# Attention's squared scores as TensorE weights, with the norm as a 129th column, and outputs normed in rows before they are transposed and projected

## What is computed

```python
qk = jnp.einsum('bthd,bshd->bhts', q, k) * scale
a = qk ** DEG                                   # DEG = 2
gate = logG[:, :, :, None] - logG[:, :, None, :]
a = jnp.where(causal, a * jnp.exp(gate), 0.0)
norm = jnp.sum(a, axis=-1) + 1e-06
y = jnp.einsum('bhts,bshd->bthd', a, v)
y = y / jnp.transpose(norm, (0, 2, 1))[..., None]
return y.reshape(B, T, H * R * D) @ Wc + bc
```

## Time and profile before

| | |
|---|---|
| median of 3 runs | 2522.14 us (2518.66 to 2523.69) |
| the profiled execution, its time | 2519.12 us |
| its span, first to last instruction | 2517.2 us |
| TensorE matmul busy | 2289.9 us, 91% |
| GpSimd busy | 1535.7 us, 61% |
| VectorE busy | 1409.0 us, 56% |
| ScalarE busy | 1221.0 us, 49% |
| mean granted TensorE clock | 0.958 |
| attention's first and last L1162/L1159 | 58.5 us and 1765.2 us |

### The profile page before, as it was taken

The page is one execution under the profiler, slowest core; times in us unless marked ns, Lnnn a source line. Parts: engine busy times, 40 slices in busy tenths (PEclk is TensorE's granted clock), DMA queues, the critical chain, the costliest instruction groups (busy, mean ns, idle before and its releaser), DMA issues.

```text
span 2517.2 us, 34737 instructions
## 1 busy us (share of the span) xinstructions
PE 2289.9 (91%) x11880; PEld 1783.5 (71%) x11880; DVE 1409.0 (56%) x3036; ACT 1221.0 (49%) x2322; POOL 1535.7 (61%) x1422
## 2 busy tenths in 40 slices
PE   5999999999999899999989999998787999999980
PEld 3777776776767677676767767666576788888870
DVE  2444444445565444556544455654653878788863
ACT  3454444444434444443444444334333677777763
POOL 2666555544568754456875445687323688888885
PEclk8999999999999999999989999999788999999995
DMA  3766722122113212211321221121443988898956
GB/s 119 299 257 243 272 101 64 40 66 67 49 52 104 84 40 66 67 49 52 104 84 40 66 66 49 52 84 52 146 155 125 273 209 206 195 218 190 216 88 219
DMA packets 152695, 310.34 MB, mean 123 GB/s; under 512 B 26528, under 2 KB 88224, under 8 KB 152512
## 3 DMA queue, kind: packets, MB, share of 16 engines
q1 hardware_dynamic: 104176, 252.05, 29.8%
q0 software_dynamic: 48192, 55.68, 11.5%
q10 hardware_dynamic: 144, 0.33, 0.0%
HBM read 168.01 MB, written 149.34 MB: 126 GB/s over the span
## 4 chain that ended last, share of the span: by engine, by line
PE 71%; DVE 8%; POOL 8%; issue 7%; ACT 4%; DMA 2%; POOLq 0%; SPq 0%; ACTq 0%; DVEq 0%
PE bank L810 44%; PE bank L1162 13%; PE bank L820 6%; PE bank L1172 3%; POOL nacc L2038 3%; POOL slots L2077 2%; PE bank L1262 2%; POOL y_part L2087 2%; PE bank L1159 1%; DVE acc L1699 1%; DVE ub L1664 1%; ACT a L1415 1%; DVE yt_lo L1678 1%; ACT yt_hi L1426 1%; DMA y_part<-y_e,row_token 1%
## 5 line engine op out<-in xcount | busy, mean ns | idle before, releaser
L2038 POOL TENSOR_TENSOR nacc<-nacc,a 128x512 f32<-128x512 f32 (+1 forms) x384 | 448.0, 1167 | 292.1 <-ACT a L1419 139.8
L1162 PE MATMUL bank<-a,v 128*128 128x512 f32 x1024 | 529.0, 598 | 5.3 <-DVE nrm L1684 4.9
L2087 POOL DMA_INDIRECT y_part<-y_e,row_token x264 | 415.9, 1575 | 103.5 <-issue 82.5
L1415 ACT ACTIVATE a<-bank,c_s 128x512 f32<-128x512 f32 x384 | 263.4, 686 | 172.7 <-PE bank L810 148.5
L810 PE MATMUL bank<-q_hi,k_hi 128*128 128x512 f32 (+1 forms) x640 | 323.8, 506 | 12.5 <-ACT a L1415 6.2
L1419 ACT ACTIVATE a<-ub 128x512 f32<-128x512 f32 (+1 forms) x256 | 133.9, 523 | 392.2 <-DVE ub L1664 374.3
L2038 POOL TENSOR_TENSOR nacc<-a,a 128x512 f32<-128x512 f32 (+1 forms) x128 | 149.0, 1164 | 258.6 <-ACT a L1415 199.0
L1699 DVE SCALAR_TENSOR_TENSOR acc<-bank,rec,acc 128x256 f32<-128x256 f32 x512 | 223.5, 478 | 95.6 <-PE bank L810 89.6
L2077 POOL DMA_INDIRECT slots<-rows,slot_u x192 | 192.5, 1003 | 137.4 <-DVE slot_u L1826 86.1
L810 PE MATMUL bank<-q_lo,k_hi 128*128 128x512 f32 (+1 forms) x640 | 240.3, 375 | 0.0
L810 PE MATMUL bank<-q_hi,k_lo 128*128 128x512 f32 (+1 forms) x640 | 238.5, 373 | 0.0
(11 more groups left out here) (217 smaller groups left out, 5666.9 us busy)
## 6 DMA issues: line engine op xcount, KB each, us to landing
slots<-acc SPq DMA_DIRECT2D x65, 816.0 KB, 7.3
w_raw_f<-in_wffn SPq DMA_DIRECT2D x66, 624.0 KB
xr<-slots SPq DMA_DIRECT2D x64, 544.0 KB
decay_all<-decay_dram SPq DMA_DIRECT2D x128, 128.0 KB
w_hi<-w_dram SPq DMA_DIRECT2D x24, 384.0 KB
w_lo<-w_dram SPq DMA_DIRECT2D x24, 384.0 KB
sum<-y_part SPq DMA_DIRECT2D x16, 512.0 KB, 9.6
wc_hi<-wc_dram SPq DMA_DIRECT2D x24, 256.0 KB
```

Of the source, the lines that this page charges most:

```text
L1162: e.matmul(dst, v[n % 3][:, s, :], a32[u % NA][:, :, :], start=first, stop=False, skip_group_check=True).then_inc(s_av)
L1415: e.activation(squares, score_bank(u)[:, 0:R * w].rearrange("p (r t) -> p r t", r=R), ACT.Square, scale=c_s[b % 2][:, g * (g - 1) + s, h:h ...
L2038: e.tensor_tensor(out_, a, b, op).then_inc(s_nadd)
L2087: e.indirect_dma_start(out=y_part[part], out_offset=bass.IndirectOffsetOnAxis(ap=token, axis=0), in_=y_e[y][:, j, :], in_offset=None, boun ...
```

## The change

The sides of the second product are exchanged. The squares `a` are the weights, 128 query tokens at a time, and the moving side is `v` with a 129th column of ones (`DN = D + 1`). A full unit is now 4 products of 129 columns (two tiles of 128 tokens times R = 2), a half is 2. Outputs come in rows, tokens on the partitions, and the 129th column is the norm. A group takes two banks, so only two groups have a place at a time (`PLACE_OF`), and a group waits until the one before it in its place was read out by `normed`. The units' order is changed for that.

Gone are GpSimd's whole `av` (`nacc`), the norm's products on TensorE, ScalarE's `decay_f` and the copy `yt` from the outputs' bank. The decay is VectorE's product with one number a row, two instructions a group (`f_t`, made once a sequence). After a group's last unit VectorE adds the epsilon, takes the reciprocal and writes the normed rows `yn`; two units later TensorE transposes them (4 transposes into a spare bank), ScalarE and VectorE split them into `yt_hi` and `yt_lo`; and two units after that the 12 products of the projection run as one task, both query heads added up in one bank, which VectorE adds to `acc` in one instruction.

```diff
-UNITS = []
-for g_ in range(1, NG):
-    UNITS += [(g_, s_) for s_ in range(2 * g_)] + [(g_ - 1, 2 * g_ - 2), (g_ - 1, 2 * g_ - 1)]
-UNITS += [(NG - 1, 2 * NG - 2), (NG - 1, 2 * NG - 1)]
+
+UNITS = ([(0, 0), (0, 1)] + [(1, 0), (1, 1)] + [(2, 0), (2, 1)] + [(1, 2), (1, 3)] + [(2, 2), (2, 3)]
+         + [(3, s_) for s_ in range(6)] + [(2, 4), (2, 5)] + [(3, 6), (3, 7)])
...
+PLACE_OF, before_in = {}, {}
+free_ = [(0, None), (1, None)]
+for n_, g_, s_ in UNITS_ALL:
+    if (n_, g_) not in PLACE_OF:
+        PLACE_OF[n_, g_], before_in[n_, g_] = free_.pop(0)
+    if s_ == 2 * g_ + 1:
+        free_.append((PLACE_OF[n_, g_], (n_, g_)))
+
+DN = D + 1
...
-            do("yt", n_, g)
-            late += [(u + 2, "norm", n_, g, 0), (u + 2, "project", n_, g, 0), (u + 3, "project", n_, g, 1)]
+            do("normed", n_, g)
+            late += [(u + TURN_BEHIND, "turn", n_, g), (u + PROJECT_BEHIND, "project", n_, g)]
...
-        return GROUP_NTH[n - 1, g] + 1 if n else 0
+        return GROUP_NTH[before_in[n, g]] + 1 if before_in[n, g] else 0
...
-        def av_bank(g):
-            return bank[2 + g]
+        def outputs(n, g):
+
+            return banks[1 + PLACE_OF[n, g]][:, :, 0:R * DN].rearrange("p t (r d) -> p t r d", r=R)
...
             def av(u):
                 n, g, s = UNITS_ALL[u]
-                first = s == 0
-                dst = av_bank(g)[:, :].rearrange("p (r t) -> p r t", r=R)
+                dst = outputs(n, g)
                 once.wait_ge(s_sq, u + 1)
                 once.wait_ge(*out_of(("val", n // PAIR, s // 2)))
-                if first:
-
-                    once.wait_ge(s_nrm, place_free(n, g))
+                once.wait_ge(s_ones, 6)
+                if s == 0:
+
+                    once.wait_ge(s_yn, place_free(n, g))
                 if s == 2 * g and g:
-                    once.wait_ge(s_off, f_nth(n, g))
-                if s == 2 * g + 1:
-                    e.matmul(dst[:, :, P:GROUP], v[n % 3][:, s, :], a32[u % NA][:, :, 0:P], start=False, stop=True,
-                             skip_group_check=True).then_inc(s_av)
-                else:
-                    e.matmul(dst, v[n % 3][:, s, :], a32[u % NA][:, :, :], start=first, stop=False,
-                             skip_group_check=True).then_inc(s_av)
-
-            def norm(n, g):
+                    once.wait_ge(s_off, nth["decay", n, g])
+                for tt in range(s - 2 * g if s > 2 * g else 0, 2):
+                    t0 = tt * P if s <= 2 * g else 0
+                    for r in range(R):
+                        ins = e.matmul(dst[:, tt, r, :], a32[u % NA][:, r, t0:t0 + P], v[n % 3][:, s, :], start=(s == 0 and r == 0),
+                                       stop=(s == 2 * g + tt), skip_group_check=True)
+                ins.then_inc(s_av)
+
+            def turn(n, g):
+                task = "turn", n, g
                 j = GROUP_NTH[n, g]
-                once.wait_ge(s_yt_lo, j + 1)
-                once.wait_ge(s_nadd, nadd_of[unit_of[n, g, 2 * g + 1]])
+                ps = bank[6 + spare[task] % 2][:, :].rearrange("p (r t) -> p r t", r=R)
+                once.wait_ge(s_yn, j + 1)
+                once.wait_ge(s_tab, 5)
+                once.wait_ge(*out_before(task))
                 for tt in range(2):
                     for r in range(R):
-                        k = tt * R + r
-                        ins = e.matmul(av_bank(g)[:, k:k + 1], nacc[g][:, r, tt * P:(tt + 1) * P], ones[:, 0:1], start=(k == 0),
-                                       stop=True, skip_group_check=True)
-                ins.then_inc(s_norm)
-
-            def project(n, g, r):
-                task = "project", n, g, r
+                        ins = e.transpose(ps[:, r, tt * P:(tt + 1) * P], yn[j % YR][:, tt, r, :], ident)
+                ins.then_inc(s_spare)
+
+            def project(n, g):
+                task = "project", n, g
                 j = GROUP_NTH[n, g]
                 ps = bank[6 + spare[task] % 2]
                 hi, lo = wc_hi[n % 2], wc_lo[n % 2]
-                once.wait_ge(s_yt_lo, j + 1)
+                once.wait_ge(*out_of(("turn", n, g)))
                 if n < H:
                     once.wait_ge(s_wc_lo, n + 1)
                 else:
...
                 for tt in range(2):
                     ts = slice(tt * P, (tt + 1) * P)
                     ins = product(e, ps[:, tt * C:(tt + 1) * C], [(yt_hi[j % 2][:, r, ts], yt_lo[j % 2][:, r, ts], hi[:, r, :],
-                                                                   lo[:, r, :])], first=(tt == 0))
+                                                                   lo[:, r, :]) for r in range(R)], first=(tt == 0))
...
-            def decay_f(n, k):
...
-                    e.activation(f_b[k - 1][:, :], decay_all[k % 2][:, 0:GROUP], ACT.Exp).then_inc(s_f)
+                e.activation(f_t[i][:, :, :], local[:, :, :], ACT.Exp)
...
-            def yt(n, g):
-                j = GROUP_NTH[n, g]
-                once.wait_ge(s_av, unit_of[n, g, 2 * g + 1] + 1)
+            def turn(n, g):
+                j, m = GROUP_NTH[n, g], spare["turn", n, g]
+                once.wait_ge(s_spare, m + 1)
                 if j >= 2:
-                    once.wait_ge(s_spare, spare[("project", *GROUPS[j - 2], R - 1)] + 1)
-                e.activation(yt_hi[j % 2][:, :, :], av_bank(g)[:, :].rearrange("p (r t) -> p r t", r=R), ACT.Copy).then_inc(s_yt_hi)
+                    once.wait_ge(s_spare, spare[("project", *GROUPS[j - 2])] + 1)
+                e.activation(yt_hi[j % 2][:, :, :], bank[6 + m % 2][:, :].rearrange("p (r t) -> p r t", r=R), ACT.Copy).then_inc(s_yt_hi)
...
             def decay(n, g):
-                part = av_bank(g)[:, :].rearrange("p (r t) -> p r t", r=R)
+                b, h = divmod(n, H)
+                part = outputs(n, g)
                 once.wait_ge(s_av, unit_of[n, g, 2 * g - 1] + 1)
-                once.wait_ge(s_f, f_nth(n, g))
-                e.tensor_tensor(part, part, f_b[g - 1][:, :].unsqueeze(1).to_broadcast([P, R, GROUP]), ALU.mult).then_inc(s_off)
-
-            def yt(n, g):
-                j = GROUP_NTH[n, g]
+                once.wait_ge(s_c, b + 1)
+                for tt in range(2):
+                    ins = e.tensor_scalar(part[:, tt, :, :], part[:, tt, :, :], f_t[b % 2][:, 2 * g + tt, h:h + 1], None, ALU.mult)
+                ins.then_inc(s_off)
+
+            def normed(n, g):
+
+                j, part = GROUP_NTH[n, g], outputs(n, g)
+                once.wait_ge(s_av, unit_of[n, g, 2 * g + 1] + 1)
+                e.tensor_scalar(nrm[:, :, :], part[:, :, :, D], NORM_EPS, None, ALU.add).then_inc(s_nrm)
+                once.wait_ge(s_nrm, j + 1)
+                e.reciprocal(rec[:, :, :], nrm[:, :, :]).then_inc(s_rec)
+                if j >= YR:
+                    once.wait_ge(s_spare, spare[("turn", *GROUPS[j - YR])] + 1)
+                once.wait_ge(s_rec, j + 1)
+                e.tensor_tensor(yn[j % YR][:, :, :, :], part[:, :, :, 0:D], rec[:, :, :].unsqueeze(3).to_broadcast([P, 2, R, D]),
+                                ALU.mult).then_inc(s_yn)
+
+            def turn_lo(n, g):
+                j, m = GROUP_NTH[n, g], spare["turn", n, g]
                 once.wait_ge(s_yt_hi, j + 1)
                 if j >= 2:
-                    once.wait_ge(s_spare, spare[("project", *GROUPS[j - 2], R - 1)] + 1)
-                e.tensor_tensor(yt_lo[j % 2][:, :, :], av_bank(g)[:, :].rearrange("p (r t) -> p r t", r=R), f32(yt_hi[j % 2][:, :, :]),
-                                ALU.subtract).then_inc(s_yt_lo)
-
-            def norm(n, g):
-                j = GROUP_NTH[n, g]
-                once.wait_ge(s_norm, j + 1)
-                e.tensor_scalar(nrm[:, :], av_bank(g)[:, 0:2 * R], NORM_EPS, None, ALU.add).then_inc(s_nrm)
-                once.wait_ge(s_nrm, j + 1)
-                e.reciprocal(rec[j % 2][:, :], nrm[:, :]).then_inc(s_rec)
-
-            def add(n, g, r):
-                m, b, j = spare["project", n, g, r], n // H, GROUP_NTH[n, g]
+                    once.wait_ge(s_spare, spare[("project", *GROUPS[j - 2])] + 1)
+                e.tensor_tensor(yt_lo[j % 2][:, :, :], bank[6 + m % 2][:, :].rearrange("p (r t) -> p r t", r=R), f32(yt_hi[j % 2][:, :, :]),
+                                ALU.subtract).then_inc(s_out_of[m % 2])
+
+            def add(n, g):
+                m, b = spare["project", n, g], n // H
                 once.wait_ge(s_spare, m + 1)
                 once.wait_ge(s_acc0, 2 * b + 2)
-                once.wait_ge(s_rec, j + 1)
-                if r:
-                    once.wait_ge(*out_of(("project", n, g, 0)))
-                elif n % H:
-                    once.wait_ge(*out_of(("project", n - 1, g, 1)))
-                for tt in range(2):
-                    part = acc[b % 2][:, 2 * g + tt, :]
-                    ins = e.scalar_tensor_tensor(out=part, in0=bank[6 + m % 2][:, tt * C:(tt + 1) * C],
```

(16 more changed lines are left out.)

125 lines of the change are left out of this document (44 added, 81 removed).

## The result

| | before | after |
|---|---|---|
| median of 4 runs | 2520.4 us (2515.36 to 2523.69) | 2430.32 us (2420.76 to 2433.14) |
| profiled execution, its span | 2519.12, 2517.2 | 2420.76, 2418.9 |
| mean granted TensorE clock | 0.958 | 0.966 |
| first and last product of attention | 58.5 and 1765.2 | 57.0 and 1670.8 |
| from there to the end | 752.0 | 748.1 |

The ratio is 0.9638 [0.9606, 0.9669], 3.6% faster. Of the 98.3 us between the profiled executions 93 lie in attention.

The account below looks back on a forecast made before the run. TensorE's own work (busy 91% of the span), then its waits in attention, were taken as the bound. From 2519.1 us, -30 (TensorE), -18 (GpSimd) and +10 (new waits) gave 2481, 2482 for a median; 8-in-10 range 2448 to 2522.

Parts of the forecast that it names:

- The norm's products: TensorE in attention: removing them from 128 groups, 0.89 us each, saves 114 us.
- The transposes: TensorE in attention: four f32 transposes a group, 128 times 0.45 us, add 58 us.
- The exchanged product: TensorE in attention: 4608 instructions of 129 columns at 0.113 us, 521 us against 495, add 26; ends +7 and +58.
- TensorE's part: Norm's products, transposes and exchanged product together: -30 us, ends -49 and +2, all on the path.
- GpSimd's relief: Dropping `nacc` ends TensorE's waits for `nacc` (13.4 us) and `nrm` (4.9): -18 us, ends 0 and -25.
- the wait of 4.59 us: A TensorE wait placed in the late stretch where GpSimd is 80% busy with `nacc` and the scatter.
- VectorE and ScalarE: VectorE's 51 us less work counts 0, having cover; the 40.2 us of `acc` waits stay; ends -15 and +15.
- The new waits: TensorE waiting for `yn` at a group's transpose or its successor's first product: +10 us, ends 0 and 46.
- Rival 1: Two places for groups: TensorE waits for `yn` at most groups; at 0.8 us each, 2574 us; chance 0.11.
- Rival 2: TensorE's weight loads don't hide: 2514 us with 0.12 an instruction (chance 0.14), 2572 with late starts too (0.04).
- Rival 4: Transposes lower TensorE's granted clock in attention; 3% is +51 us, 2533 us; chance 0.03.
- Rival 3: Routed sequences near the first's pace: a third of some 60 us more, no new wait, 2452 us; chance 0.18.

Follow-up runs that it names:

- one_turn: The changed kernel with one of each group's four transposes, three left out; 2598.37 us, 1.0304, its experts' part distorted by uneven routing of tokens.
- half_cols: The changed kernel moving 65 instead of 129 columns in every unit but a group's first; 2349.9 us, ratio 0.9471.
- no_sums: The kernel before with GpSimd's sums of squares left out and `nacc` a constant, the norm's products kept; 2427.93 us, ratio 0.9783.
- sums_back: The changed kernel with GpSimd's sums put back as work nobody reads, holding the tiles `a` until added; ratio 0.9667.
- before_again: The kernel before, unchanged, run again on a chip of the faster kind; 2479.62 us, ratio 1.0003.
- after_again: The changed kernel as it is, run again on a chip of the faster kind; 2352.71 us, ratio 0.9484.
- two_adds: The kernel before with two of the four additions to `acc` in each group left out; ratio 0.9908.
- four_adds: The changed kernel with the projection added to `acc` by four instructions of 256 columns instead of one of 512; ratio 0.9687.
- old_pace: The changed kernel with the next head's columns spread evenly over the units instead of at places named by hand; ratio 0.9586.
- paced_again: The changed kernel with each scatter piece waiting for TensorE's unit at its place, on a chip of the slower kind; 2388.65 us, ratio 0.949.
- after_control: The changed kernel as it is, control on the same slower-kind chip as paced_again; 2426.12 us, ratio 0.962.
- one_norm: The kernel before with one of the norm's four products in each group, three left out; ratio 0.9835.

## Why the prediction was right in its sign and wrong in its size

- **The norm's products, -114: held**, -117.
- **The transposes, +58: held**, +56; one_turn gives 0.106 each, and the trace 0.43 us for four against the 0.45 of the forecast.
- **The exchanged product, +26: right in kind, 12 us too dear**, +14. I took 0.113 an instruction; it is 0.111, the norm's own price. half_cols shows that the number of columns does not matter. TensorE's part was forecast at -30, and is -47, within its ends of -49 and +2.
- **GpSimd's relief, -18 with ends 0 and -25: mis-sized.** 44 to 47 us by no_sums and sums_back. I counted only waits that name GpSimd, and those went (17 us on the chip of before_again). The waits for `ub` and `log_g` that hang on it were left out, 8 us, and the clock that is low after a wait was an end of 7 us; no_sums shows 41 us less at half speed, 20 us. One reading was also wrong, without harm to the sum: the wait of 4.59 us, at 1719.78, lies outside the stretch of the earlier trace rows that I put it in.
- **VectorE and ScalarE, 0, ends -15 and +15: the step that failed.** The sentence was that the waits for `acc` "come from routing work ahead of the addition, which stays". The waits fell from 44.9 us in attention to 20.3, and to 15.2 on the chip of after_again. More than half of them was time in the additions themselves (24.2 us) and a third in routing (14.3), and neither stayed. A bank is free at the end of the addition that reads it: two of 478 ns, twice a group, became one of 690. two_adds shows that half their length is worth 18 us of attention in the kernel before, four_adds that holding one bank for all four costs 50 in the changed one, where the ends allowed 15. How the gain divides between shorter additions and the later places of the tasks stays open, but for the columns below. The cover that I named (45 to 47 of 100 us busy in the first sequence) says nothing of a chain that holds one of two banks.
- **The placing of the columns, not priced at all:** 26 us by old_pace, of which 16 are waits for `acc`. It is a part of the edit that my description of the change left out.
- **The new waits, +10: too many.** `yn` cost 0.7 us. `yt_lo` was already there, 3.5 us in attention, and is 2.8 without stalls and 8.3 with them.
- **What was missing on the other side:** the bursts of the scatter, 37 us on the chip of the recorded result (paced_again against after_control). Without them the result would be some 2393 us, and the forecast off by 89 us and not by 52.

The single parts, 50 + 26 + 44 for what they cost when undone, make 120 us, and undone together they cost 114. That is more than the 86 us that attention lost in idle time and low clock (55 + 31) on the way from before_again to after_again. four_adds holds a bank twice as long as the kernel before did; what else fills the gap is open. one_norm shows that with two bounds of like height the worth of a part depends on the rest: 86 us of products gave 41. The sum of the forecast, one engine's work plus the waits that carry a name, has no place for that.

**The rivals.** Rival 1, the two places: refuted, 0.7 us. Rival 2, the weight path: refuted. The next product does start 0.08 us late behind the eight (151.00 to 151.31, against 0.23), but the eight started closer by as much, and the 0.111 contains it. Rival 4, the clock: refuted, the mean rose from 0.958 to 0.966. Rival 3, more relief: right in mechanism, and its "third of some 60 us" was too little; on the undisturbed chip attention's idle time fell by 55 of 80 us.

## What to carry to other kernels

Price a shared buffer's release by the end of the instructions that read it out and by what stands ahead of them on their engine, not by the busy share of that engine. Where an engine is 90% busy and still waits, look for a second bound of the same height, and value a change to both as one, since what is taken from one alone comes back in part as waits. When an engine is freed, look at what it issues next: pace its bursts with a wait on the work they belong to.

## What the runs showed of the hardware

- Chips differ by 40 us (1.6%) in the same program: 2480 on two, 2520 on two others, all of it behind attention. TensorE's waits that the trace puts to "issue" are 1.9 us on one of the first kind (before_again) and 28.9 on one of the second (before), which is most of it.
- A series of indirect DMAs from GpSimd at 1.28 us each goes with stops of TensorE and ScalarE of 1 to 2 us on chips of the second kind and not on the first: 37 us between after_control and paced_again.
- Kernels that stop less spend less time at 1.2 GHz: 68 us of attention before (80.6 us idle), 27 after (47.8), 7 with the scatter paced (25.9). On top of each idle us that left came 0.6 us from the clock on this way; between other pairs it was from 0.1 (four_adds against after_again) to 0.8 (before_again against no_sums).
- A plain f32 instruction with a 128x128 weight takes 0.111 us with 1, 65 or 129 columns.
- VectorE's instructions take as long beside GpSimd's sums as without them: 478 ns for an addition to `acc` in before and in no_sums.
